# Up products of the last network as three f32r products, with weights split once on chip

## The reference

```
x = x + tanh(g_xattn[0]) * mixer(ctx, layernorm(x))       # conv, 16-state selective scan, D skip, silu(z) gate
x = x + tanh(g_ffn[0])   * bit_ffn(layernorm(x), w1, w2)  # 512 -> 2048 -> 512, quantised
x = x + tanh(g_xattn[1]) * (layernorm(x) @ attention(ctx))
x = x + tanh(g_ffn[1])   * ffn(layernorm(x))
# the last network:  h = gelu(x @ proj1.T + b1);  out = h @ proj2.T + b2      512 -> 2048 -> 512, float32
```

## Time and profile before

| | us |
|---|---|
| median of 3 runs | 972.18 (970.7 to 974.12) |
| the profiled execution's own time | 973.76 |
| its span, first to last instruction | 971.6 |
| busy: PE / DVE / ACT / POOL | 819.5 / 761.6 / 649.5 / 518.9 |

### The profile page before, as it was taken

One profiled execution on the slowest core, in us unless ns is written; L12 is line 12 of the kernel. 1 busy time (PEld: TensorE's weight loads), 2 busy tenths in 40 slices (PEclk: granted clock), 3 DMA queues, 4 the chain that ended last, 5 costly groups with the idle time before them and its releaser, 6 DMA issues. The chain is left out here.

```text
span 971.6 us, 9284 instructions
## 1 busy us (share of the span) xinstructions
PE 819.5 (84%) x2770; PEld 406.0 (42%) x2810; DVE 761.6 (78%) x895; ACT 649.5 (67%) x968; POOL 518.9 (53%) x456
## 2 busy tenths in 40 slices
PE   6721247799799999999799999998899999898999
PEld 2210013354344344454344444444343444446887
DVE  4589997885889998975899998966899998754333
ACT  4599979473699973674699863672799862614442
POOL 0699786102899884003999882014998881012000
PEclk9755558799899999999899999989899999999999
DMA  8079983001299965301399963301599961201231
GB/s 299 11 142 208 269 200 58 1 1 44 38 194 236 235 143 150 108 2 44 78 206 244 237 137 94 109 1 43 115 221 205 238 142 54 109 1 44 88 108 65
DMA packets 46816, 119.54 MB, mean 123 GB/s; under 512 B 5792, under 2 KB 6944, under 8 KB 46256
## 3 DMA queue, kind: packets, MB, share of 16 engines
q0 software_dynamic: 16128, 58.73, 32.2%
q1 hardware_dynamic: 30640, 60.24, 18.4%
HBM read 56.03 MB, written 4.19 MB: 62 GB/s over the span
## 5 line engine op out<-in xcount | busy, mean ns | idle before, releaser
L1651 POOL TENSOR_TENSOR work<-du,bcast 128x1024 f32<-128x1024 f32 x128 | 353.8, 2786 | 23.9 <-ACT bcast L875 23.3
L1269 DVE TENSOR_TENSOR_SCAN pair<-pair,work 128x512 f32<-128x512 f32 x256 | 299.3, 1215 | 34.2 <-ACT pair L890 30.0
L890 ACT ACTIVATE pair<-dt,a_neg 128x512 f32<-128x512 f32 x256 | 165.8, 682 | 20.2 <-DVE work L1276 17.2
L661 PE MATMUL bank<-stage,ring 128*128 128x512 f32 x384 | 172.9, 593 | 5.9 <-ACT bcast L875 4.4
L1276 DVE TENSOR_TENSOR work<-pair,ccast 128x1024 f32<-128x1024 f32 x128 | 156.8, 1225 | 11.6
L1666 POOL DMA_DIRECT2D u<-work x112 | 122.9, 1097 | 36.5 <-DVE work L1276 17.1
L1637 POOL TENSOR_SCALAR fst<-fst 128x1 f32<-128x1 f32 x32 | 9.3, 291 | 207.3 <-DVE fst L1496 207.0
L445 PE MATMUL bank<-xd,pick 128*128 128x512 bf16 x108 | 48.0, 445 | 82.9 <-ACT bcast L875 56.6
L661 PEld LDWEIGHTS bank<-stage,ring 128*128 128x128 f32 x384 | 71.8, 190 | 80.4 <-issue 70.9
L675 PE MATMUL bank<-ring,stage 128*128 128x512 f32 x192 | 85.6, 594 | 1.7 <-ACT hx L1149 1.7
L445 PEld LDWEIGHTS bank<-xd,pick 128*128 128x128 bf16 x128 | 13.1, 102 | 140.7 <-ACT bcast L875 90.2
(11 more groups left out here) (168 smaller groups left out, 1500.0 us busy)
## 6 DMA issues: line engine op xcount, KB each, us to landing
u<-work POOLq DMA_DIRECT2D x112, 512.0 KB, 5.8
ring<-ffn_dram SPq DMA_DIRECT2D x120, 256.0 KB, 4.9
ring<-ffn_dram SPq DMA_DIRECT2D x16, 512.0 KB, 3.3
xres<-x_dram SPq DMA_DIRECT2D x4, 1024.0 KB, 5.4
stage<-w_dram SPq DMA_DIRECT2D x1, 4096.0 KB, 17.1
stage<-w_dram SPq DMA_DIRECT2D x4, 1024.0 KB, 7.4
out_dram<-stage SPq DMA_DIRECT2D x16, 256.0 KB, 2.1
ctxT<-ctxT_dram SPq DMA_DIRECT2D x4, 512.0 KB, 6.3
```

Of the source, the lines that this page charges most:

```text
L661: last = pe.matmul(banks[2 + f % 2][:], piece(b, f)[:, k * P:(k + 1) * P], xnT[:, k, :], start=k == 0, stop=k == J - 1)
L890: act.activation(pairs[s % DECAYBUFS][:, q, :], dt[:, p * HALF + q, :], ACT.Exp, scale=a_neg[:, p * HALF + q, n:n + 1]).then_inc(s_decay, 1)
L1269: dve.tensor_tensor_scan(pair[:, q, :], pair[:, q, :], rows[:, q, :], 0.0, ALU.mult, ALU.add).then_inc(s_scan, 1)
L1651: pool.tensor_tensor(work[:, s % SCANBUFS, :, :], du[:, p * HALF:(p + 1) * HALF, :], bcast[:, n % 2, :].unsqueeze(1).broadcast_to([P, HALF ...
```

## The change

- In the middle passes an up is now, for each of the four k, three f32r products: high weights by high rows, high weights by low rows, low weights by high rows. `norm_copy` of the later norm writes the high rows (`x_high`, f32r) and no longer `xnT`; DVE subtracts them from PSUM for the low rows (`x_low`), four instructions per pass in slot 4. The first up waits for the last of them.
- The weights are split once: SP loads all of proj1 (four chunks of 1 MB) in pass 0; ACT copies each chunk to f32r (`high_part`, 128x2048, at the end of pass 0, after `W_LATE` and before `turning`); POOL subtracts in place (`low_parts`, four times 128x2048, at the head of pass 1, before `between`); SP stores both parts in a DRAM tensor, from which each middle pass loads 512 KB per up.
- Six of the ups have places of their own (`home_*`, in `hT`, `stage` and `hx`), and are loaded ahead of slot 5 with four more in the ring.
- Ups go to three banks (2, 3, 1), and there are five per slot: one each at places 0, 1 and 2 and two at place 3. The downs begin at slot 8, place 2, all 16 pairs lie in slots 8 to 12, and none is left in `turning`. `fourth` of r = 0 moves from slot 11 to slot 10.

```diff
-FFN_UP = {(5 + f // 4, f % 4): f for f in range(FT)}
-FFN_DOWN = {(9, 0): (0, 0), (9, 1): (0, 2), (9, 2): (0, 4), (10, 0): (0, 6), ..., (12, 3): (1, 10)}
-FOURTH_SLOTS = {(11, 0): 0}
+UP_BANKS = (2, 3, 1)
+FFN_UP = {(5, 0): (0,), (5, 1): (1,), (5, 2): (2,), (5, 3): (3, 4), (6, 0): (5,), (6, 1): (6,), (6, 2): (7,), (6, 3): (8, 9),
+          (7, 0): (10,), (7, 1): (11,), (7, 2): (12,), (7, 3): (13, 14), (8, 0): (15,)}
+FFN_DOWN = {(8, 2): (0, 0), (8, 3): (0, 2), (9, 0): (0, 4), (9, 1): (0, 6), (9, 2): (0, 8), (9, 3): (0, 10), (10, 0): (0, 12), (10, 1): (0, 14),
+            (10, 3): (1, 0), (11, 0): (1, 2), (11, 1): (1, 4), (11, 2): (1, 6), (11, 3): (1, 8), (12, 0): (1, 10), (12, 1): (1, 12), (12, 2): (1, 14)}
+FOURTH_SLOTS = {(10, 2): 0}
...
             def run(b, more, context_after):
                 if more:
-                    for k in range(PIECES):
-                        load_piece(b, k)
+                    for f in (6, 7, 8, 9, 0, 1, 4, 2, 3, 5):
+                        load_up(b, f)
...
+            for c in range(4):
+                sp.dma_start(raw_up(c)..., ffn_d[c * CHUNK:(c + 1) * CHUNK, :, 0:D]...).then_inc(s_rawup[c], 16)
+            for c in range(4):
+                keep_up(c)
+            for c in (3, 0, 1, 2):
+                keep_low(c)
...
             def energies(b, prev, j):
                 else:
                     pe.wait_ge(s_qk, b * 2 + 2)
+                    if prev is not None:
+                        pe.wait_ge(s_fgelu, prev * FT + FT)
...
                 gate_transposes(m, (2,))
-                f_pair(b, 1, 12)
-                f_pair(b, 1, 14)
                 q_transposes(m, (0,))
...
             def f_up(b, f):
-                if f >= 2:
-                    pe.wait_ge(s_fgelu, b * FT + f - 1)
+                if f >= 3:
+                    pe.wait_ge(s_fgelu, b * FT + f - 2)
+                elif f == 2:
+                    pe.wait_ge(s_qk, (b + 1) * 2 + 2)
                 else:
-                    pe.wait_ge(s_xnTc, b * 2 * T + 2 * T)
-                pe.wait_ge(*loaded(b, f))
+                    pe.wait_ge(s_xlow, b * T + T)
+                pe.wait_ge(*up_loaded(b, f))
+                parts = up_parts(b, f)
                 for k in range(J):
-                    last = pe.matmul(banks[2 + f % 2][:], piece(b, f)[:, k * P:(k + 1) * P], xnT[:, k, :], ...)
+                    ks = slice(k * P, (k + 1) * P)
+                    last = product(banks[UP_BANKS[f % 3]], ((parts[:, 0, ks], x_high[:, k, :]), (parts[:, 0, ks], xnT_low[:, k, :]),
+                                                            (parts[:, 1, ks], x_high[:, k, :])), k == 0, k == J - 1)
...
+            def high_part(c):
+                act.wait_ge(s_rawup[c], 16)
...
+                act.activation(in_parts(high_up(c)), raw_up(c), ACT.Copy).then_inc(s_uphigh, 1)
...
+            def x_low(b, t):
+                ts = slice(t * P, (t + 1) * P)
+                dve.wait_ge(s_xnTc, b * 2 * T + T + t + 1)
+                dve.tensor_tensor(in_parts(xnT_low[:, :, ts]), banks[2 + t % 2][:]..., x_high[:, :, ts],
+                                  ALU.subtract).then_inc(s_xlow, 1)
...
                     if rest and slot == 4:
                         norm_apply(b, 6)
                         norm_apply(b, 7)
+                        x_low(b, 0)
+                        x_low(b, 1)
                     half(m, prev, slot, 0, 1)
-                    if rest and (slot, 0) in FOURTH_SLOTS:
-                        fourth(b, FOURTH_SLOTS[slot, 0])
+                    if rest and slot == 4:
+                        x_low(b, 2)
+                        x_low(b, 3)
                     half(m, prev, slot, 1, 0)
+                    if rest and (slot, 2) in FOURTH_SLOTS:
+                        fourth(b, FOURTH_SLOTS[slot, 2])
...
+            def low_parts():
+                for c in (3, 0, 1, 2):
+                    pool.wait_ge(s_uphigh, c + 1)
+                    raw = raw_up(c)
+                    pool.tensor_tensor(in_parts(raw), raw, high_up(c), ALU.subtract).then_inc(s_uplow[c], 1)
+                pool.wait_ge(s_kept[2], 32)
+                pool.wait_ge(s_kept[3], 32)
```

More of the change, by code:

```diff
@@ L36 @@
 PIECES = 8
-LOADS = 2 * FT + PIECES
+HOMES = 6
+CHUNK = FT // 4
 PAD = TAPS - 1
@@ L155, in program @@
         wstat = sb("wstat", [P, 2, 4])
-        ring = sb("ring", [P, PIECES, D])
+        with ExitStack() as here_first:
+            ring = sb_in(here_first, "ring", [P, PIECES, D])
+        ring_up = sb("ring_up", [P, PIECES, D])
         ctxT = sb("ctxT", [P, KC, L])
@@ L544, in up1, with attention @@
                     last.then_inc(s_mm1, 1)
-            def attention(b, slot, which, p):
+            def attention(b, prev, slot, which, p):
                 done = att_step(slot, which, p, ATT_EVERY)
@@ L679, in f_unit @@
             def f_unit(b, slot, place):
-                if (slot, place) in FFN_UP:
-                    f_up(b, FFN_UP[slot, place])
+                for f in FFN_UP.get((slot, place), ()):
+                    f_up(b, f)
                 if (slot, place) in FFN_DOWN:
@@ L815, in pass_ @@
                         keep_awake(16)
-                    attention(m, slot, 0, 0)
+                    attention(m, prev, slot, 0, 0)
                     if slot == QK_SLOT:
@@ L823, in pass_ @@
                     bcast_next(m, slot, 0, 1)
-                    attention(m, slot, 0, 1)
+                    attention(m, prev, slot, 0, 1)
                     if slot == QK_SLOT:
@@ L832, in pass_ @@
                     bcast_next(m, slot, 1, 0)
-                    attention(m, slot, 1, 0)
+                    attention(m, prev, slot, 1, 0)
                     if rest:
@@ L836, in pass_ @@
                     bcast_next(m, slot, 1, 1)
-                    attention(m, slot, 1, 1)
+                    attention(m, prev, slot, 1, 1)
                     if rest:
@@ L1148, in f_gelu @@
                 act.wait_ge(s_fmm1, b * FT + f + 1)
-                act.activation(h_tile(f), banks[2 + f % 2][:], ACT.Gelu, bias=b1[:, f:f + 1]).then_inc(s_fgelu, 1)
+                act.activation(h_tile(f), banks[UP_BANKS[f % 3]][:], ACT.Gelu, bias=b1[:, f:f + 1]).then_inc(s_fgelu, 1)
             def f_gelus(b, slot, place):
                 for i in (place, place + 1):
-                    if (slot, i) in FFN_UP:
-                        f_gelu(b, FFN_UP[slot, i])
+                    for f in FFN_UP.get((slot, i), ()):
+                        f_gelu(b, f)
             def pass_(b, rest=True):
```

188 lines of the change are left out of this document (127 added, 61 removed).

## The result

The changed kernel takes 1013.39 us (median of 4 runs, 1011.63 to 1016.76); on the same chip the kernel before took 972.52. The ratio is 1.0409, 95% interval 1.0383 to 1.0435: 41 us slower, where I had forecast 21. The profiled execution has a span of 1011.1 us against 971.6, so the traces account for 39.5.

The account below looks back on a forecast made before the run. It took the last-closing loop, ACT's with PE in the up stage and DVE's from slot 9, as the bound. Three passes at +4.5 (13.5), splitting +8 and closing -0.5 gave +21, a median of 993 us, range 980 to 1005.

Parts of the forecast that it names:

- What bounds: Whole kernel: three engines are close, the loop that closes last counts; 34 us less PE work does not shorten the scan.
- Slot 4: Start of a middle pass's ups: low rows on DVE make the Gelus of ups 0 and 1 later, +0.6 (0.6 to 1.5).
- Half slots: Slots 5 to 7: 7.45 us with two ups, 9.72 with three; a slot of five ups costs +1.7 on 15.46.
- Second half of slot 5 +2.0: Slot 5 of each middle pass: its second half was forecast to make the pass 2.0 us later.
- PE's downs ... end about 1 us before DVE comes to `fourth`: From slot 8, place 2: eight pairs of downs at 3.43 us, broadcasts and attention finish about 1 us before `fourth`.
- the gate: End of each middle pass's scan: DVE's 2.78 us wait for the gate transposes falls to about 0.7, so -2.1.
- Turning: After each middle pass's gate: -0.35 without the two pairs of downs, +2.1 (0 to 3) for the cooled clock.
- warm in turning: Rival for the turning: PE stays warm there, 993 - 6 = 987 us; chance 0.17.
- Splitting: Between pass 0 and the first middle pass: POOL's four subtractions hold up DVE's tensor_scalars, +8 (3 to 13).
- hidden: Rival for the weight splitting: it costs nothing visible, 985 to 988 us; chance 0.12.
- In `closing` one ACT copy ... is gone: -0.5: Closing, between the last transposes and the first product: one ACT copy fewer was forecast to save 0.5 us.
- Transfers bind: Rival from slot 8, place 2: with a 230 GB/s ceiling, transfers cost up to +9, 1002 us; chance 0.13.

Follow-up runs that it names:

- e4: Changed kernel with the places of ups, downs and `fourth` of the kernel before, two pairs of downs in the turning again; 987.30 us, ratio 1.0136.
- e12: e5 with POOL's subtractions cut to 128 of 2048 columns, so most low parts of the weights are left out; 974.57 us, ratio 1.0004 to the kernel before.
- e6: Changed kernel, still five ups per slot, but two at place 2 and one at place 3 instead of one and two; 993.34 us, ratio 1.0195.
- e2: Changed kernel with useless matmuls on TensorE ahead of and between broadcasts of slots 5 and 8, to keep it warm; 1000.75 us, ratio 1.0289.
- e1: Changed kernel; in the closing alone, the low rows of tiles 0 and 1 are made on DVE ahead of the last norms; 1010.33 us, ratio 1.0375.
- e5: Changed kernel with the edits of e1 and e4 together: the old places and the closing's new order; 982.72 us, ratio 1.0094.

## Why the prediction was wrong

The sign was right, with its main reason; the time lies outside the range. By its steps:

- **What bounds.** Right. 34 us less of ups bought 1.5 us per pass in slots 5 to 8, and the low rows took them: e4's second and third middle passes stand at 0, e12 at 1.0004.
- **Slot 4.** 0.9, 1.5 and 1.1 for +0.6 (0.6 to 1.5): within its bounds, at the upper end.
- **Half slots.** Right in structure and size at a full clock: 7.45 and 9.72 forecast, 7.41 and 9.90 measured; slots 6 and 7 cost 1.85 and 1.86 (1.7). e6 shows the cause. The sum left out 0.28 us that the first half of slot 5 should save by the same 7.45.
- **"Second half of slot 5 +2.0".** Mis-sized: 3.1, and 1.5 where it is kept warm (e2). The step failed at the clock. I priced the two ups behind the broadcast at 2.72 us each, though my own walk says that TensorE waits for ACT's copy ahead of them. I had rows for what follows such a wait in the turning, and did not ask for it here.
- **"PE's downs ... end about 1 us before DVE comes to `fourth`".** Failed. With one up in slot 8 TensorE idles three times, cools, and the first pair of downs takes 6.2 us (331.68 to 337.90) for the 3.43 forecast. DVE loses 2.6 us from half step 19 to 29, partly in waits for broadcasts (ACT waits 2.38 us for the one it copies at 338.32). With slot 8 at -1.16 (-1.15) and the gate at -1.88 (-2.1) nearly as forecast, the first pass comes to +7.4 and not +2.75; e2 shows that the clock is 4.4 us of these, nearly the whole difference.
- **Turning.** 1.4 and 1.3 for the clock (2.1), -0.26 and +0.10 for the downs (-0.35); from the gate to the projection +1.43 and +1.65 (+1.75). What I had not seen is that the next stage passes on all of it once (+1.47) and nothing the other time (-0.01). The rival "warm in turning" is out by 0.53.
- **Splitting.** Right in the mechanism: the tensor_scalars take 2.40, 8.16 and 2.84 us, as in the walk. In size +6.5 for +8; the other 1.3 of the first middle pass's lateness were there before, in pass 0. That it is 6.5 and not 9 to 10, as in five kernels with the same code there, is luck. The rival "hidden" is out.
- **"In `closing` one ACT copy ... is gone: -0.5".** Failed, +6.3. I counted the ACT copy that is taken away and not what it did: it emptied the bank for the next transposes. Now DVE's x_low empties it (four of them, as before), and the first stood behind a norm that waits for POOL, and so ahead of the transposes. That is 5.1 us in this kernel (e1), of which about half is the clock that falls in the gap: where it stays up, the order is worth 2.5 (e4 to e5). It is the mistake that I had avoided in slot 4.
- **Transfers bind.** Out: slots 9 and 10 move 259 GB/s, over the 230 that the rival set as a ceiling, and TensorE is busy there for 15.00 of 15 us; from 338 to 392 it waits for no transfer.
- **Tail.** Taken as unchanged, +1.2: products every 0.2325 us for 0.227, cause open.

Of the 18.5 us by which the traces differ from my sum, 14.6 lie in the slots (some 12.5 of them the clock, by e2) and 6.2 in the closing and the tail; the turnings cost 2 less than I took. The boundary's 1.5 less and pass 0's 1.3 more nearly cancel.

## What to carry to other kernels

When an engine that does not close the loop becomes cheaper, moving its work into fewer places is not free: count what stands behind the handshake in each place, not the sum over a slot. A gap of 1 to 2 us on TensorE can cost twice, as the gap and as the work behind it at half clock: price both, and look how much of that work is on the path. Where it is, a few useless matmuls can cost less. And these subtractions on POOL were DVE's time too, in long pieces and in short; take such work away and see, before moving it.

## What the runs showed that I had not expected

- TensorE's clock fell to mostly the lower of its two levels (1.2 of 2.4 GHz) after a single idle time of 2.06 us (slot 5), or 0.88 and 1.31 us and during a third of 1.61 (slot 8); in e6 the same slot 5 without such a gap kept 1.00, and so did slots 6 and 7 with gaps of 0.88 to 1.22 us, one per half slot.
- Cutting POOL's instructions in four does not spare DVE: quantising fell from 8.16 to 2.92 us, and six convolution instructions rose from 4.55 to 10.01. POOL loses too: its subtractions take 23.5 us and not 18.5.
- Shifts of one or two microseconds early in a program change later stages by up to 3, through where the clock falls: the boundary cost 6.5 us in four kernels and 9.0 to 10.1 in five with the same code there. Edits worth less than that have to be read from the stretch where they lie, not from the total.
